# A low-rank adaptive layer and a recurrence on one core: the prologue from B2 on in another order, and x's first 64 steps on ScalarE's queue

## Chip, cores and metric

The kernel runs on one core of a Trainium2 chip. The metric is the device time of one execution in microseconds (us). Three timed runs of the kernel before gave a median of 525.01 us (524.35 to 525.34).

## What is computed

Four sequences (B = 4) of T = 512 steps and D = 256 features go through a layer whose low-rank factors are made from a condition vector, and then through a tanh recurrence; both add their input. The reference, cut to what matters (the layer's result takes the place of x ahead of the recurrence):

```python
c = layernorm(cond) * gamma + beta
w = gelu(c @ W1 + bias1) @ W2 + bias2                 # 4 x 8192
a1, b1, a2, b2 = [t.reshape(B, D, 8) for t in split(w, 4, axis=-1)]
u   = einsum('btd,bdr->btr', x, a2)
mid = gelu(x @ base_down + einsum('btr,blr->btl', u, b2))
v   = einsum('blr,btl->btr', b1, mid)
x   = x + (x + mid @ base_up.T + einsum('bkr,btr->btk', a1, v))
h_t = tanh(x_t @ Wx + b + h_(t-1) @ Wh)               # 512 steps, one after the other
out = x + h
```

## The kernel before

Every engine has a program written out by hand, and semaphores order them; there is no scheduler. The kernel has two stages.

**The recurrence** fills nearly all of the time. Two pairs of 16 steps (`PAIR` = 32) make one round; each step (`state_products`, L938) multiplies the state, split in three bf16 parts, by the parts of Wh in 24 matmuls, ScalarE takes the tanh (L494), VectorE makes the lower parts of the new state (`residue`, L579 and L583). In the gap in which TensorE would wait for the tanh stand other products: the layer for the next 32 steps (`fill_product`), the next inputs (`input_product`), transposes of x's rows. In the last 16 steps two matmuls (`x2_last_rows`, L862) put the last 8 rows of the layer's result where the output is summed; `X2_LAST` says from which step.

**The prologue** is all that must be done ahead of the first tanh (L494). It makes the four factors from W2, 8 MB, in the order A2, B2, B1, A1. For each factor j there are two halves c, and for each half two transfers k of 512 KB. `bias_product(j, c)` (L702) starts a bank with bias2; `w_products(j, c)` (L723) waits for the transfer of each k and adds 4 products, one for each strip of 32 partitions. VectorE's `keep_rank` (L559, L562) masks the result and reduces it to the compact factor `fac[j]`. A2 and B1 are turned by TensorE (`turn_factor`, L732). B2 and A1 are laid out by VectorE's `spread` (L566) as the block matrices `b2d` and `a1d` (128 x 256), from which a product of full height is made:

```python
nc.tensor.matmul(columns(bank[4 + n][:, 0:B * BL]), a1d[:, P * n:P * (n + 1)], v0_sb[:], start=False,
                 stop=True, skip_group_check=True).then_inc(up_psum, 1)
```

The order on TensorE is: x's first 64 steps transposed (`first_transposes`, L710, behind a wait for `ld_x[0]`), bias1 (L759), `cn` transposed (L763), the hidden layer (L773), x times base_down (L716), A2 and B2's products, u (L796), base_up turned (L802), the b2 products into mid (L808), B1's products, mid times base_up (L739), B1 turned, step 0 of the recurrence with h0 (L938), v (L743), A1's products, the a1 product (L749), the input products of the first tile (L831). `keep_busy(n)` (L689) puts n products of zeros, whose result nobody reads, between them.

All large loads are issued by SyncE (SP) on its queue, in the order x's first 64 steps, W1, base_down, A2, B2, Wh, base_up, B1, Wx, A1, and straight behind these x's other rows (`xb_sb` for steps 64 to 127, then three transfers of 512 KB, L317). Six small ones are issued by ScalarE.

Of the kernel before, what the change touches and what calls it, by code (L numbers as in the profile page):

```python
# [24 lines left out]
P = 128  # L25
# [7 lines left out]
def adaptive_lowrank_then_recurrence(nc, x, cond, base_up, base_down, ln_gamma, ln_beta, W1, bias1, W2,  # L33
# [25 lines left out]
    with ExitStack() as ctx:  # L59
# [240 lines left out]
        EARLY_SUMS, X2_LAST, EARLY_TURN, EARLY_ROWS = TS - LAST + 1, 9, 11, 12  # L300
# [12 lines left out]
        def _(sp):  # L313
# [11 lines left out]
            sp.dma_start(x_sb[0:T0, :, 0], x[:, 0:T0].rearrange("b p d -> p b d")).then_inc(ld_x[0], 16)  # L325
# [8 lines left out]
            load_w2(A1)  # L334

# [188 lines left out]
        def _(dve):  # L524
# [65 lines left out]
            keep_rank(B2, 0)  # L590
            spread(b2d, B2, 0).then_inc(b2d_ready, 1)
# [61 lines left out]

            def residues(pair, first, last):
                for s in range(PAIR):
# [28 lines left out]
        def _(pe):  # L684
# [33 lines left out]

            def w_products(j, c):
                for k in range(K2):  # L720
                    pe.wait_ge(ld_w2[j][c][k], 16)
                    for e in range(NCH):
                        last = nc.tensor.matmul(wbank(j, c)[Q * e:Q * (e + 1), :],  # L723
                                                gRep[:, k].rearrange("p b r -> p (b r)"),
                                                w2_sb[:, k, j, HC * (NCH * c + e):HC * (NCH * c + e + 1)], start=False,
                                                stop=(k == K2 - 1), skip_group_check=True)
                last.then_inc(w_ready[j], 1)
# [334 lines left out]
```

## Time and profile before

| what | us |
|---|---|
| three timed runs, median | 525.01 |
| the profiled execution's own time | 524.89 |
| its span, first to last instruction | 523.1 |
| first tanh of the recurrence | 37.44 |
| TensorE (PE) busy, share of the span | 505.3, 97% |
| VectorE (DVE) busy, share | 290.7, 56% |
| ScalarE (ACT) busy, share | 175.5, 34% |
| GpSimd (POOL) busy, share | 22.0, 4% |

The profile is of one execution. PE is TensorE's matmuls, PEld its weight loads, SPq and ACTq the issues of transfers by SyncE and ScalarE. Times in a trace count from the first instruction. A matmul in f32 is two instructions, so that `x16` in a row is 8 matmuls. A busy time of PE holds overlapping matmuls; the chain of waits gives what each group added.

### The profile page before, as it was taken

What the parts mean: (1) busy time and instruction counts of PE and PEld (TensorE: products, weight loads), DVE (VectorE), ACT (ScalarE), POOL (GpSimd) and SP (SyncE); (2) the same over time, 40 slices, a digit from 0 to 9 for tenths busy, and PEclk for the clock granted to TensorE, in tenths of its full rate; (3) what the DMA queues carried; (4) which work ended last, traced back from release to release, by engine and by line L of the source; (5) the groups of instructions that cost most, each with busy time, mean ns of one, the idle gap of its engine ahead of it and who ended that gap; (6) DMA issues with size and microseconds to landing.
All of it is one profiled execution on the core that took longest, in us unless ns stands there. A gap on an engine that the chain in (4) does not pass through costs nothing.

```text
span 523.1 us, 33150 instructions
## 1 busy us (share of the span) xinstructions
PE 505.3 (97%) x14760; PEld 471.2 (90%) x14760; DVE 290.7 (56%) x2274; ACT 175.5 (34%) x1159; POOL 22.0 (4%) x35
## 2 busy tenths in 40 slices
PE   9999999999999999999999999999999999998987
PEld 6569999999999999999999999999999999997885
DVE  2545565565556556555655555565655655565554
ACT  3103333333333333333333333333333333333322
POOL 7350000000000000000000000000000000000000
PEclk9999999999999999999999999999999999999999
DMA  8970000000000000000000000000000000000000
GB/s 295 398 217 4 4 14 4 5 14 4 14 5 14 4 9 11 4 14 4 15 4 14 4 5 14 5 14 4 14 4 4 14 4 14 4 14 4 5 14 13
DMA packets 8026, 16.05 MB, mean 31 GB/s; under 512 B 540, under 2 KB 5708, under 8 KB 7884
## 3 DMA queue, kind: packets, MB, share of 16 engines
q1 hardware_dynamic: 7816, 13.90, 7.8%
q8 instruction: 115, 1.88, 1.5%
q14 instruction: 27, 0.22, 0.1%
q10 hardware_dynamic: 68, 0.05, 0.0%
HBM read 11.85 MB, written 2.10 MB: 27 GB/s over the span
## 4 chain that ended last, share of the span: by engine, by line
PE 95%; ACT 3%; issue 1%; DVE 1%; POOL 0%; DVEq 0%; POOLq 0%
PE bank L938 64%; PE bank L842 7%; PE bank L904 4%; PE bank L885 4%; ACT h_ring L494 3%; PE bank L909 2%; PE bank L899 2%; PE bank L880 2%; PE bank L890 2%; PE bank L689 2%; PE bank L723 2%; PE bank L851 1%; PE bank L702 1%; PE bank L826 1%; PE bank L926 1%
## 5 line engine op out<-in xcount | busy, mean ns | idle before, releaser
L938 PE MATMUL bank<-h_ring,whp 128*128 128x52 bf16 x6132 | 243.6, 186 | 12.7 <-ACT h_ring L494 12.7
L579 DVE TENSOR_TENSOR r_ring<-h_ring 128x4 f32<-128x4 f32 x1022 | 136.0, 163 | 206.1 <-ACT h_ring L494 203.6
L494 ACT ACTIVATE h_ring<-bank 128x4 f32<-128x4 f32 x1022 | 141.9, 174 | 318.9 <-PE bank L938 311.1
L938 PEld LDWEIGHTS bank<-h_ring,whp 128*128 128x128 bf16 x6132 | 188.3, 96 | 34.7 <-ACT h_ring L494 25.7
L938 PE MATMUL bank<-r_ring,whp 128*128 128x52 bf16 x4096 | 219.5, 185 | 0.0
L938 PEld LDWEIGHTS bank<-r_ring,whp 128*128 128x128 bf16 x4096 | 173.6, 96 | 0.0
L938 PE MATMUL bank<-l_ring,whp 128*128 128x52 bf16 (+1 forms) x2048 | 156.4, 178 | 0.0
L583 DVE TENSOR_TENSOR l_ring<-r_ring 128x4 bf16<-128x4 f32 x1024 | 135.7, 162 | 0.0
L938 PEld LDWEIGHTS bank<-l_ring,whp 128*128 128x128 bf16 x2048 | 121.5, 96 | 0.0
L842 PE MATMUL bank<-xp,wxp 128*128 128x32 bf16 x1488 | 63.0, 176 | 0.0
L842 PEld LDWEIGHTS bank<-xp,wxp 128*128 128x128 bf16 x1488 | 50.5, 95 | 0.0
L904 PE MATMUL bank<-mid,upT 128*128 128x128 f32 x120 | 28.0, 316 | 0.0
L885 PE MATMUL bank<-xT,down_sb 128*128 128x128 f32 x112 | 26.2, 316 | 0.0
L826 PE MATMUL bank<-ones,b3h 128*128 128x32 bf16 x128 | 22.4, 176 | 0.0
L904 PEld LDWEIGHTS bank<-mid,upT 128*128 128x128 f32 x120 | 17.9, 188 | 0.0
L885 PEld LDWEIGHTS bank<-xT,down_sb 128*128 128x128 f32 x112 | 16.7, 188 | 0.0
L627 DVE TENSOR_TENSOR y_sb<-x2T,h_ring 128x64 f32<-128x64 f32 (+1 forms) x64 | 15.3, 279 | 0.0
L909 PE MATMUL bank<-v_sb,a1d 128*128 128x128 f32 x60 | 14.0, 316 | 0.0
L899 PE MATMUL bank<-mid,b1T 128*128 128x128 f32 x60 | 14.0, 316 | 0.0
L880 PE MATMUL bank<-xT,a2T 128*128 128x128 f32 x56 | 13.1, 316 | 0.0
L890 PE MATMUL bank<-u_sb,b2d 128*128 128x128 f32 x56 | 13.1, 316 | 0.0
L826 PEld LDWEIGHTS bank<-ones,b3h 128*128 128x128 bf16 x128 | 12.2, 96 | 0.2 <-issue 0.2
(134 smaller groups left out, 241.7 us busy)
## 6 DMA issues: line engine op xcount, KB each, us to landing
w_sb<-in_L_cond_W SPq DMA_DIRECT2D x16, 512.0 KB, 11.5
out<-o_sb SPq DMA_DIRECT2D x15, 128.0 KB
x_sb<-in_x SPq DMA_DIRECT2D x3, 512.0 KB, 15.6
x_sb<-in_x SPq DMA_DIRECT2D x1, 256.0 KB, 3.9
w_sb<-in_L_cond_W SPq DMA_DIRECT2D x1, 256.0 KB, 3.8
down_sb<-in_L_cond_base_down SPq DMA_DIRECT2D x1, 256.0 KB, 5.2
wh_sb<-in_L_cond_Wh SPq DMA_DIRECT2D x1, 256.0 KB, 11.4
up_sb<-in_L_cond_base_up SPq DMA_DIRECT2D x1, 256.0 KB, 11.6
```

The source lines that it names most:

```text
L494: nc.scalar.activation(state, zt, ACT.Tanh).then_inc(h_ready, 1)
L579: nc.vector.tensor_tensor(r_ring[:, k, q, 0:B], state_before(pair, s, k)[:, 0:B], state_hi_before(pair, s, k)[:, 0:B], ALU.subtract).then_ ...
L583: nc.vector.tensor_tensor(l_ring[:, k, q, 0:B], r_ring[:, k, q, 0:B], r_hi[:, k, q, 0:B], ALU.subtract).then_inc(l_ready, 1)
L826: nc.tensor.matmul(zbank(p, q, m)[:, 0:TC // 2], b3h[:, P * m:P * (m + 1)], ones[:], start=True, stop=False, skip_group_check=True)
L842: nc.tensor.matmul(zb, wxp[w][:, k, P * m:P * (m + 1)], rhs, start=False, stop=False, skip_group_check=True)
L880: ins = nc.tensor.matmul(columns(fill_out(tile, 0)), a2T[:, k].rearrange("p e q -> p (e q)"), xT[:, k, :, t0:t0 + BL], start=(k == 0), sto ...
L885: nc.tensor.matmul(columns(fill_out(tile, 1 + c)), down_sb[:, k, P * c:P * (c + 1)], xT[:, k, :, t0:t0 + BL], start=(k == 0), stop=False)
L890: nc.tensor.matmul(columns(fill_out(tile, 1 + c)), b2d[:, P * c:P * (c + 1)], u_sb[:], start=False, stop=True).then_inc(fmid_psum, 1)
L899: ins = nc.tensor.matmul(columns(fill_out(tile, 0)), b1T[:, k].rearrange("p e q -> p (e q)"), rhs, start=(k == 0), stop=(k == K2 - 1))
L904: nc.tensor.matmul(columns(fill_out(tile, 1 + c)), upT[:, k, P * c:P * (c + 1)], rhs, start=(k == 0), stop=False)
L909: nc.tensor.matmul(columns(fill_out(tile, 1 + c)), a1d[:, P * c:P * (c + 1)], v_sb[:], start=False, stop=True).then_inc(fup_psum, 1)
L938: return nc.tensor.matmul(zbank(p, q, m)[:, col0:col0 + n], whp[part][:, k, P * m:P * (m + 1)], rhs[:, 0:n], start=False, stop=stop, skip_ ...
```

## The change

1. x's first 64 steps are issued by ScalarE as its fourth transfer, not by SP as its first.
2. SP waits for A1's last two transfers ahead of x's other rows.
3. On TensorE 29 products of zeros (`keep_busy`) go from six places from B2 on, and 3 take the place of 7 ahead of B1's turning. The bias products of B1 and A1 no longer stand in pairs. B2's second half stands ahead of u and base_up's turning.
4. The first b2 and a1 products take the compact factor: `strip_products` makes 4 products of 32 rows by 32 columns in place of one of 128 by 128. The spreads of `a1d` and `b2d` stand in steps 3, 5, 6 and 7 of the recurrence on VectorE.
5. `state_products` is split in two; its second part for step 0 stands between A1's last products and the input products. The a1 product of the first half stands between A1's last two quarters.
6. `x2_last_rows` makes 64 columns at a time, in steps 3 to 6 of the last 16, not 128 in steps 9 and 10.

```diff
@@ -297,7 +297,7 @@
-        EARLY_SUMS, X2_LAST, EARLY_TURN, EARLY_ROWS = TS - LAST + 1, 9, 11, 12
+        EARLY_SUMS, X2_LAST, EARLY_TURN, EARLY_ROWS = TS - LAST + 1, 3, 11, 12
...
@@ -322,7 +322,6 @@
-            sp.dma_start(x_sb[0:T0, :, 0], x[:, 0:T0].rearrange("b p d -> p b d")).then_inc(ld_x[0], 16)
...
@@ -332,6 +331,9 @@
+
+            sp.wait_ge(ld_w2[A1][1][0], 16)
+            sp.wait_ge(ld_w2[A1][1][1], 16)
...
@@ -419,6 +421,7 @@
+            act.dma_start(x_sb[0:T0, :, 0], x[:, 0:T0].rearrange("b p d -> p b d")).then_inc(ld_x[0], 16)
...
@@ -587,26 +590,25 @@
-            keep_rank(B2, 0)
-            spread(b2d, B2, 0).then_inc(b2d_ready, 1)
+            for c in range(2):
+                keep_rank(B2, c)
             dve.wait_ge(u_psum, 1)
             nc.vector.tensor_tensor(u0_sb[:], bank[6][:, 0:B * T0].rearrange("p (b t) -> p b t", b=B),
                                     bmask[:].unsqueeze(2).broadcast_to([P, B, T0]), ALU.mult).then_inc(u_ready, 1)
-            keep_rank(B2, 1)
-            spread(b2d, B2, 1).then_inc(b2d_ready, 1)
             residue(0, 0)
-            keep_rank(B1, 0)
-            keep_rank(B1, 1)
+            for c in range(2):
+                keep_rank(B1, c)
             dve.wait_ge(b1T_psum, 2)
             nc.vector.tensor_copy(b1T[:, 1], turned(1)).then_inc(b1T_ready, 1)
+            keep_rank(A1, 0)
             dve.wait_ge(v0_psum, 1)
             nc.vector.tensor_tensor(v0_sb[:], bank[6][:, 0:B * BL].rearrange("p (b t) -> p b t", b=B),
                                     bmask[:].unsqueeze(2).broadcast_to([P, B, BL]), ALU.mult).then_inc(v0_ready, 1)
-            for n in range(K2):
-                keep_rank(A1, n)
-                spread(a1d, A1, n).then_inc(a1d_ready, 1)
-                dve.wait_ge(up_psum, n + 1)
-                make_x2(n, 0, TS).then_inc(x2_first, 1)
+            dve.wait_ge(up_psum, 1)
+            make_x2(0, 0, TS).then_inc(x2_first, 1)
+            keep_rank(A1, 1)
+            dve.wait_ge(up_psum, 2)
+            make_x2(1, 0, TS).then_inc(x2_first, 1)
...
@@ -650,6 +652,13 @@
+
+
+            PLACING = {3: (a1d, A1, 0, a1d_ready), 5: (a1d, A1, 1, a1d_ready), 6: (b2d, B2, 0, b2d_ready),
+                       7: (b2d, B2, 1, b2d_ready)}
+
+            def place(dst, j, c, done):
+                spread(dst, j, c).then_inc(done, 1)
...
@@ -665,6 +674,8 @@
+                    if tile == 0 and i in PLACING:
+                        place(*PLACING[i])
...
@@ -745,9 +759,17 @@
+
+            def strip_products(j, n, rhs, ncol, done):
+                for e in range(NCH):
+                    rows = slice(Q * e, Q * (e + 1))
+                    last = nc.tensor.matmul(columns(bank[4 + n][rows, 0:ncol]), fac[j][rows, n], rhs[rows], start=False,
+                                            stop=True, skip_group_check=True)
+                last.then_inc(done, 1)
+
             def a1_first_product(n):
-                nc.tensor.matmul(columns(bank[4 + n][:, 0:B * BL]), a1d[:, P * n:P * (n + 1)], v0_sb[:], start=False,
-                                 stop=True, skip_group_check=True).then_inc(up_psum, 1)
+                pe.wait_ge(fac_ready[A1], n + 1)
+                strip_products(A1, n, v0_sb, B * BL, up_psum)
...
@@ -785,39 +807,36 @@
-            keep_busy(4, 7)
             w_products(B2, 0)
             pe.wait_ge(fac_ready[A2], 2)
             turn_factor(A2, a2T_psum)
-            for c in range(2):
-                bias_product(B1, c)
+            bias_product(B1, 0)
+            w_products(B2, 1)
             pe.wait_ge(a2T_ready, 2)
             for k in range(K2):
                 last = nc.tensor.matmul(columns(bank[6][:, 0:B * T0]), a2T[:, k].rearrange("p e q -> p (e q)"),
                                         xT[:, k, :, 0:T0], start=(k == 0), stop=(k == K2 - 1))
             last.then_inc(u_psum, 1)
-            w_products(B2, 1)
             pe.wait_ge(ld_up, 16)
             for i in range(K2 * K2):
                 last = nc.tensor.transpose(bank[7][:, P * i:P * (i + 1)],
                                            up_sb[:, i % K2, P * (i // K2):P * (i // K2 + 1)], ident[:])
             last.then_inc(upT_psum, 1)
+            bias_product(B1, 1)
             pe.wait_ge(u_ready, 1)
             for m in range(K2):
-                pe.wait_ge(b2d_ready, m + 1)
-                nc.tensor.matmul(columns(bank[4 + m][:, 0:B * T0]), b2d[:, P * m:P * (m + 1)], u0_sb[:], start=False,
-                                 stop=True, skip_group_check=True).then_inc(mid_psum, 1)
-                keep_busy(4, 6)
+                pe.wait_ge(fac_ready[B2], m + 1)
+                strip_products(B2, m, u0_sb, B * T0, mid_psum)
             w_products(B1, 0)
-            for c in range(2):
-                bias_product(A1, c)
+            bias_product(A1, 0)
             pe.wait_ge(upT_ready, 1)
             for n in range(K2):
                 for k in range(K2):
                     pe.wait_ge(mid_ready, max(n, k) + 1)
                     base_up_product(n, k)
             w_products(B1, 1)
-            keep_busy(7, 7)
+            bias_product(A1, 1)
+            keep_busy(3, 6)
...
@@ -858,9 +877,10 @@
-            def x2_last_rows(k):
-                nc.tensor.matmul(last_rows(k), x2T[:, k, (T - LAST) * B:T * B], ident[:], start=True, stop=False,
-                                 skip_group_check=True)
+            def x2_last_rows(k, h):
+                cols = slice(P // 2 * h, P // 2 * (h + 1))
+                nc.tensor.matmul(last_rows(k)[:, cols], x2T[:, k, (T - LAST) * B:T * B], ident[:, cols], start=(h == 0),
+                                 stop=False, skip_group_check=True)
...
@@ -1011,28 +1038,24 @@
-            state_products(0, 0)
+            high_products(0, 0)
+            w_products(A1, 0)
             pe.wait_ge(b1T_ready, 2)
             for k in range(K2):
                 v0_product(k)
-            w_products(A1, 0)
-            keep_busy(6, 7)
+            w_half_products(A1, 1, 0)
             pe.wait_ge(v0_ready, 1)
-            pe.wait_ge(a1d_ready, 1)
             a1_first_product(0)
-            w_products(A1, 1)
+            w_half_products(A1, 1, 1)
+            rest_products(0, 0)
             pe.wait_ge(ld_wx, 16)
             pe.wait_ge(x2_first, 1)
             for m in range(K2):
                 first_input_product(0, m, 0)
-            bias_start(0, 1, 0)
-            first_input_product(1, 0, 0)
-            keep_busy(8, 7)
-            pe.wait_ge(a1d_ready, 2)
             a1_first_product(1)
-            bias_start(0, 1, 1)
-            first_input_product(1, 1, 0)
-            keep_busy(3, 7)
+            for m in range(K2):
+                bias_start(0, 1, m)
+                first_input_product(1, m, 0)
```

TensorE's order from B2's first products to those of B1's first half, before (`w_sb` is W2, `zeros` are the products of `keep_busy`, `b2d` the spread factor):

```order
L723 MATMUL bank<-w_sb,gRep 32x256 x8
L732 MATMUL bank<-ident,fac 32x128 x8
L702 MATMUL bank<-bias_sb,quadrant 128x256 x2
L796 MATMUL bank<-xT,a2T 128x256 x2
L723 MATMUL bank<-w_sb,gRep 32x256 x8
L802 MATMUL bank<-ident,up_sb 128x128 x4
L808 MATMUL bank<-u_sb,b2d 128x256
L689 MATMUL bank<-zeros 128x256 x4
L808 MATMUL bank<-u_sb,b2d 128x256
L689 MATMUL bank<-zeros 128x256 x4
L723 MATMUL bank<-w_sb,gRep 32x256 x8
```

and now (`fac` beside `u_sb` is the compact factor):

```order
L733 MATMUL bank<-w_sb,gRep 32x256 x8
L746 MATMUL bank<-ident,fac 32x128 x8
L713 MATMUL bank<-bias_sb,quadrant 128x256
L733 MATMUL bank<-w_sb,gRep 32x256 x8
L817 MATMUL bank<-xT,a2T 128x256 x2
L822 MATMUL bank<-ident,up_sb 128x128 x4
L713 MATMUL bank<-bias_sb,quadrant 128x256
L766 MATMUL bank<-u_sb,fac 32x256 x8
L733 MATMUL bank<-w_sb,gRep 32x256 x8
```

The 8 products of zeros in these rows are gone (so are 4 ahead of them); B2's second half has moved ahead of u, and the two b2 products have become 8 small ones in a row.

TensorE's order from A1's first products into the input products of the first tile, before (v, L743, stood ahead of these rows, and all of step 0 ahead of v):

```order
L723 MATMUL bank<-w_sb,gRep 32x256 x8
L689 MATMUL bank<-zeros 128x256 x6
L749 MATMUL bank<-v_sb,a1d 128x128
L723 MATMUL bank<-w_sb,gRep 32x256 x8
L831 MATMUL bank<-x2T,wx_sb 128x32 x2
L826 MATMUL bank<-ones,b3h 128x32
L831 MATMUL bank<-x2T,wx_sb 128x32
L689 MATMUL bank<-zeros 128x256 x8
L749 MATMUL bank<-v_sb,a1d 128x128
L826 MATMUL bank<-ones,b3h 128x32
L831 MATMUL bank<-x2T,wx_sb 128x32
L689 MATMUL bank<-zeros 128x256 x3
```

and now:

```order
L733 MATMUL bank<-w_sb,gRep 32x256 x8
L757 MATMUL bank<-mid,b1T 128x128 x2
L733 MATMUL bank<-w_sb,gRep 32x256 x4
L766 MATMUL bank<-v_sb,fac 32x128 x4
L733 MATMUL bank<-w_sb,gRep 32x256 x4
L958 MATMUL bank<-r_ring,whp 128x52 x6
L958 MATMUL bank<-l_ring,whp 128x52 x2
L958 MATMUL bank<-r_ring,whp 128x52 x2
L958 MATMUL bank<-l_ring,whp 128x52 x2
L850 MATMUL bank<-x2T,wx_sb 128x32 x2
L766 MATMUL bank<-v_sb,fac 32x128 x4
L845 MATMUL bank<-ones,b3h 128x32
```

The 17 products of zeros are gone, v stands behind A1's first half, A1's second half is cut by the first a1 product, and the second part of step 0 (L958) stands behind it. Only the first part of step 0 is still ahead of these rows.

VectorE's order from B1's turned half to the last of the layer's first result, before:

```order
L601 COPY b1T<-bank 128x128
L603 TENSOR_TENSOR v_sb<-bank,bmask 128x128
L559 TENSOR_TENSOR wmul<-bank,rmask 128x256
L562 TENSOR_REDUCE fac<-wmul 128x32
L566 TENSOR_TENSOR a1d<-fac,qmask 128x128
L571 SCALAR_TENSOR_TENSOR x2T<-xT,bank 128x4x16
L559 TENSOR_TENSOR wmul<-bank,rmask 128x256
L562 TENSOR_REDUCE fac<-wmul 128x32
L566 TENSOR_TENSOR a1d<-fac,qmask 128x128
L571 SCALAR_TENSOR_TENSOR x2T<-xT,bank 128x4x16 x3
```

and now:

```order
L602 COPY b1T<-bank 128x128
L562 TENSOR_TENSOR wmul<-bank,rmask 128x256
L565 TENSOR_REDUCE fac<-wmul 128x32
L605 TENSOR_TENSOR v_sb<-bank,bmask 128x128
L574 SCALAR_TENSOR_TENSOR x2T<-xT,bank 128x4x16
L562 TENSOR_TENSOR wmul<-bank,rmask 128x256
L565 TENSOR_REDUCE fac<-wmul 128x32
L574 SCALAR_TENSOR_TENSOR x2T<-xT,bank 128x4x16 x3
```

The two spreads stand no longer between a factor and its product, and A1's first factor is made ahead of `v_sb`.

## Rows read from the trace of the kernel before

**Rows 1.** The page, the chain that ended last: share of the span by line.

```profile
PE bank L938 64%; PE bank L842 7%; PE bank L904 4%; PE bank L885 4%; ACT h_ring L494 3%; PE bank L909 2%; PE bank L899 2%; PE bank L880 2%; PE bank L890 2%; PE bank L689 2%; PE bank L723 2%; PE bank L851 1%; PE bank L702 1%; PE bank L826 1%; PE bank L926 1%
```

**Rows 2.** Chain in order of time, prologue: start us, us, what.

```profile
6.30 0.64 PE bank L710 x8
...
15.62 0.54 PE bank L689 x4
16.16 1.00 PE bank L723 x16
17.16 0.44 PE bank L732 x16
17.60 1.06 PE bank L702 x4
18.66 1.06 PE bank L796 x4
...
25.74 1.09 PE bank L739 x8
...
34.72 0.56 PE bank L831 x4
```

**Rows 3.** Timeline, PE, the a1 product: start us, us, then what.

```profile
33.26 0.46 PE L749 MATMUL bank<-v_sb,a1d 128*128 128x128 f32 x2 [0.66 <-DVE a1d L566]
```

**Rows 4.** Timeline, ACT, the first tanh.

```profile
37.44 0.40 ACT L494 ACTIVATE h_ring<-bank 128x4 f32<-128x4 f32 x2 [7.78 <-PE bank L831]
```

**Rows 5.** Timeline, DVE, A1's second half.

```profile
35.25 0.42 DVE L562 TENSOR_REDUCE fac<-wmul 128x32 f32<-128x256 f32 x1
35.70 0.29 DVE L566 TENSOR_TENSOR a1d<-fac,qmask 128x128 f32<-128x128 f32 x1
36.67 0.53 DVE L571 SCALAR_TENSOR_TENSOR x2T<-xT,bank 128x64 f32<-128x64 f32 x3 [0.68 <-PE bank L749]
```

**Rows 6.** Timeline, SPq, issues of A1's second and last transfer.

```profile
15.12 1.47 SPq L322 DMA_DIRECT2D w_sb<-in_L_cond_W  x1
...
17.11 0.43 SPq L322 DMA_DIRECT2D w_sb<-in_L_cond_W  x1
```

**Rows 7.** DMA issues, us to landing: the same two; x's first 64 steps.

```profile
w_sb<-in_L_cond_W SPq DMA_DIRECT2D x1, 512.0 KB, 12.6
...
w_sb<-in_L_cond_W SPq DMA_DIRECT2D x1, 512.0 KB, 14.0
...
x_sb<-in_x SPq DMA_DIRECT2D x1, 256.0 KB, 3.9
```

**Rows 8.** Timeline, ACTq and POOL: the load of b on ScalarE's queue.

```profile
2.44 0.26 ACTq L423 DMA_DIRECT2D b_rows<-in_L_cond_b  x1
...
6.19 0.39 POOL L399 CAST b_part<-b_rows 3x256 bf16<-3x256 f32 x1 [1.88 <-DMA b_rows<-in_L_cond_b]
```

**Rows 9.** DMA queues, 5 to 6 us (q1 SP, q10 ScalarE): packets, MB, share.

```profile
q1 hardware_dynamic: 192, 0.33, 100.9%
q10 hardware_dynamic: 29, 0.03, 8.6%
```

**Rows 10.** Timeline, PE, the first products of zeros.

```profile
0.99 3.60 PE L689 MATMUL bank<-zeros 128*128 128x256 bf16 x16 [0.99 <-POOL zeros L364]
...
4.82 1.48 PE L689 MATMUL bank<-zeros 128*128 128x256 bf16 x12
```

**Rows 11.** Windows: us, PE, PEld, DVE, ACT, POOL busy, PEclk, DMA, GB/s.

```profile
5.07:13.00 7.93, 7.93 (x70) 6.11 (x67) 2.13 (x8) 2.16 (x7) 6.14 (x9) 1.00 1.03 394
```

**Rows 12.** Timeline, PE, the last steps.

```profile
512.05 0.47 PE L938 MATMUL bank<-h_ring,whp 128*128 128x52 bf16 x12 [0.17 <-ACT h_ring L494]
...
513.00 0.47 PE L938 MATMUL bank<-h_ring,whp 128*128 128x52 bf16 x12 [0.17 <-ACT h_ring L494]
...
513.70 0.41 PE L862 MATMUL bank<-ident,x2T 128*32 128x128 f32 x2
514.04 0.47 PE L938 MATMUL bank<-h_ring,whp 128*128 128x52 bf16 x12
```

More of the change, by code:

```diff
@@ L717, in base_down_product, with w_half_products @@
                                  start=(k == 0), stop=False, skip_group_check=True)
+            def w_half_products(j, c, k):
+                pe.wait_ge(ld_w2[j][c][k], 16)
+                for e in range(NCH):
+                    last = nc.tensor.matmul(wbank(j, c)[Q * e:Q * (e + 1), :], gRep[:, k].rearrange("p b r -> p (b r)"),
+                                            w2_sb[:, k, j, HC * (NCH * c + e):HC * (NCH * c + e + 1)], start=False,
+                                            stop=(k == K2 - 1), skip_group_check=True)
+                if k == K2 - 1:
+                    last.then_inc(w_ready[j], 1)
             def w_products(j, c):
                 for k in range(K2):
[L721 to L727, printed above, removed]
+                    w_half_products(j, c, k)
             def turn_factor(j, done):
@@ L908, in fill_product @@
                         pe.wait_ge(fv_ready, blk)
+                    if c == 0 and blk == 1:
+                        pe.wait_ge(a1d_ready, K2)
                     nc.tensor.matmul(columns(fill_out(tile, 1 + c)), a1d[:, P * c:P * (c + 1)], v_sb[:], start=False,
@@ L928, in turn_rows, with state_product, high_products, rest_products @@
                 last.then_inc(rows_psum, 1)
-            def state_products(pair, s):
+            def state_product(pair, s, part, k, m, rhs, stop=False):
                 p, q = s // TS, s % 2
                 col0 = B * (s % TS // 2)
+                n = B if stop else W
+                return nc.tensor.matmul(zbank(p, q, m)[:, col0:col0 + n], whp[part][:, k, P * m:P * (m + 1)],
+                                        rhs[:, 0:n], start=False, stop=stop, skip_group_check=True)
+            def high_products(pair, s):
+                for k in range(K2):
+                    pe.wait_ge(h_ready, 2 * PAIR * pair + 2 * s + k + 1)
+                    for m in range(K2):
+                        for part in range(NPART):
+                            state_product(pair, s, part, k, m, state_hi_before(pair, s, k))
+            def rest_products(pair, s):
+                q = s % 2
                 done = 2 * PAIR * pair + 2 * s
                 closes = not (pair == 0 and s == 0)
-                def product(part, k, m, rhs, stop=False):
-                    n = B if stop else W
-                    return nc.tensor.matmul(zbank(p, q, m)[:, col0:col0 + n], whp[part][:, k, P * m:P * (m + 1)],
-                                            rhs[:, 0:n], start=False, stop=stop, skip_group_check=True)
-                for k in range(K2):
-                    pe.wait_ge(h_ready, done + k + 1)
-                    for m in range(K2):
-                        for part in range(NPART):
-                            product(part, k, m, state_hi_before(pair, s, k))
                 pe.wait_ge(r_ready, done + 1)
@@ L959, in state_products @@
                 for part in range(2):
-                    product(part, 1, 1, r_hi[:, 1, q, :])
-                product(0, 0, 1, l_ring[:, 0, q, :])
-                ins = product(0, 1, 1, l_ring[:, 1, q, :], stop=closes)
+                    state_product(pair, s, part, 1, 1, r_hi[:, 1, q, :])
+                state_product(pair, s, 0, 0, 1, l_ring[:, 0, q, :])
+                ins = state_product(pair, s, 0, 1, 1, l_ring[:, 1, q, :], stop=closes)
                 if closes:
@@ L972, in recurrence @@
                     if not (first and s == 0):
-                        state_products(pair, s)
+                        high_products(pair, s)
+                        rest_products(pair, s)
                     else:
@@ L998, in recurrence @@
                             input_product(1 - p, n)
-                    if last and p == 1 and X2_LAST <= i < X2_LAST + K2:
-                        x2_last_rows(i - X2_LAST)
+                    if last and p == 1 and X2_LAST <= i < X2_LAST + 2 * K2:
+                        x2_last_rows(*divmod(i - X2_LAST, 2))
                     if last and p == 1 and EARLY_TURN <= i < EARLY_TURN + K2:
```

12 lines of the change are left out of this document (8 added, 4 removed).

## The prediction

> **What bounds the kernel now.** I read the chain of waits by line first: matmuls of the recurrence hold 64% of it [rows 1], and the change touches these in the last 16 steps only. So I went to the prologue, which is over with the first tanh at 37.44 us [rows 4], and read the chain there in order of time. TensorE is on it nearly throughout, and of that time some is products of zeros, which make nothing: 0.54 us for four [rows 2]. The rest of the chain is VectorE's, where a spread factor is waited for: the a1 product stood idle 0.66 us for it [rows 3]. Then I asked what holds the prologue once that goes: the transfers. A1's second transfer was issued at 15.12 and landed 12.6 later, at 27.7; its last at 17.11 plus 14.0, at 31.1 [rows 6, 7]. TensorE used that last one at 33.7 (34.72 less a group of 1.00 [rows 2]), so data was not yet the bound, but it is near.
>
> **The change part by part.**
>
> *x's first 64 steps.* TensorE waits for them at 6.30 [rows 2] and before that wait has nothing to spare. Before, they were first in SP's queue and landed 3.9 us after issue [rows 7]. Now ScalarE issues them one issue ahead of b's, so at about 2.1 [rows 8], in the midst of W1, base_down and A2. Lower end: 3.9 us again, 6.0, no wait. Upper end: b's 3 KB, issued at 2.44, came only at 6.19 [rows 8], 3.7 us; behind such a start x's 256 packets of 1 KB, 16 on each DMA engine, take turns with SP's. In 5 to 6 us the two queues ran side by side, 29 packets of q10 with 192 of q1 [rows 9]. If each of x's waits for one 4 KB packet of W2, the two move 16 x 16 x 5 KB = 1.3 MB, 3.3 us at 394 GB/s [rows 11], and land at 2.1 + 3.7 + 3.3 = 9.1. I take 7.7, near the middle: some of W1's and base_down's packets are as short as x's. TensorE then starts its transposes 1.4 us late, and all work of its own behind them moves by 1.4. ScalarE's issue itself (0.76 us for SP before) moves the statistics of the norm by as much; the wait for x covers it, and without that wait it would cost up to 0.76. bias1, b and bias2 land behind x; bias1 is needed two groups of TensorE work later, b only by GpSimd, which has Wh to wait for anyway.
>
> The Trainium skill, DMA: Bandwidth & Descriptors, "Queues, rings and completion order", says that an engine drains a packet of some 9 to 17 descriptors of one ring before it turns to the next; by that x would be through in a turn or two and the sum would be that of the first rival. The same page says that issuing from two engines saves only issue time, which the sum has as well.
>
> *The order from B2 on.* From 15.62 the work of TensorE up to A1's last product is now, with the groups of [rows 2]: six groups of W2 products at 1.00 = 6.0; four bias products at 0.53 = 2.1; two turnings at 0.44 = 0.9; u 1.06; base_up turned, half as much as the 1.09 of its product, 0.5; the b2 products, two at about 0.5, 1.0; mid times base_up 1.09; three products of zeros 0.4; the bias and first part of step 0, 12 matmuls, about 0.5 [rows 12]; v, half of u's columns, 0.5; the first a1 product 0.4 [rows 3]. Sum 14.4. Two short waits for VectorE stay (B1's factor ahead of its turning, v ahead of a1), 0.5 together. So A1's last product ends at 15.6 + 14.4 + 0.5 = 30.5, plus the 1.4 for x: 31.9.
>
> *The floor under it.* SP no longer issues x's other rows on A1's heels. Without them two more transfers of 512 KB take 1.3 us each at 394 GB/s, so A1's last lands at 27.7 + 2.7 = 30.4, not 31.1 [rows 6, 7, 11]; its four products then end at 30.9. That is 1.0 ahead of TensorE's own work: with x at 7.7 the data does not bind. It binds only if x costs less than 0.4.
>
> *Behind A1.* The last product ended at 34.72 [rows 2] and the tanh started at 37.44: 2.72. VectorE's factor (to 35.25 + 0.42 = 35.67 [rows 5]) takes 0.95; the spread of 0.29 goes, and with it what stood between it and the product; a1 about 0.4; from the result's first operation at 36.67 [rows 5] to the tanh 0.77, hardly shorter, since four input products (0.56 for two pairs [rows 2]) now stand there. About 2.25. The first tanh: 31.9 + 2.25 = 34.15, against 37.44 a gain of 3.3.
>
> *Moved to the recurrence.* Four spreads of 0.29 stand on VectorE in steps of 0.94 to 0.95 (512.05 to 513.00 [rows 12]), in which it is busy 56%; they stand behind the residues of their step, and the next tanh covers them. From nothing to 4 x 0.29 = 1.2 us; I take nothing, since that engine does as long an operation in other steps. Their readers are at step 8 and in the next 16. x's other rows are issued from 30.4; steps 64 to 127 should land 3.9 later [rows 7] with one more issue, at 35.2, and are wanted in step 4, 34.15 + 4 x 0.94 = 37.9: 2.7 spare. SP has nothing else to issue until the first output.
>
> *The end.* The two steps with an x2 product are 1.04 apart (513.00 to 514.04), not 0.95: that product keeps TensorE 0.34 from 513.70 [rows 12]. With 64 columns a quarter to a third of this goes, and the four steps fit: 0.2 us gained, at worst nothing.
>
> *Sum.* 3.3 + 0.2 = 3.5 us off the profiled execution of 524.89 (span 523.1 and 1.8 around it): 521.4. Its own time is 0.1 below the median of the timed runs, so I leave it there.
>
> **Rivals.**
> *x lands early, by 6.7.* For it: 3.9 us in the row of before. Then the data binds: tanh at 30.9 + 2.25 = 33.2, 4.4 us gained in all, 520.5. Against it: b's small load took 3.7 with 3 KB. Chance 0.14.
> *TensorE's clock falls in the wait for x.* Before, the granted clock was 1.00, the upper of the two levels of 2.4 and 1.2 GHz [rows 11], and TensorE never idled for over 0.7 us; the first 16 products of zeros took 3.60 us, the next 12 1.48 [rows 10], 0.225 against 0.123 each, so the lower level doubles a product. Now it stands for 1.4 us, soon after the clock rose, and 33 products of zeros are gone. Each microsecond of work done at the lower level costs one more. With half of the work up to the hidden layer (3.6 us) 1.8: 523.2; with all of it 525.0, no gain. Chance 0.14, a third of it at the far end.
> *The strips run one after another: slower.* The change makes a b2 or a1 product of four that differ in rows of the array as well as in columns. For their running together: 16 instructions of the W2 products, in four column strips, take 1.00, and four of full width with as many columns 1.06 [rows 2]. Strips that differ in rows this kernel has nowhere. The Trainium skill, TensorEngine Tiling (Array Packing), "Gotcha 1: PSUM Pressure", says that different row tiles cannot access the same PSUM bank at the same time, and here all four write one bank; by that rule this rival holds. In its favour from the rows: nothing; against it, that the strips write different partitions, as the column strips do. Price: a b2 product takes 4 x 0.53 = 2.1 for 0.5, an a1 product 4 x 0.27 = 1.1 for 0.4; 2 x 1.6 + 2 x 0.7 = 4.6 more. 521.4 + 4.6 = 526.0. It decides for slower from 3.5 us more on, so from about three quarters of that price. Chance 0.07.
> *The gain is taken elsewhere.* x at the late end, 9.1, and a spread or two not hidden: 1.4 + 0.6 more, 523.4; with VectorE's waits longer than 0.5 up to 524.8. Chance 0.07.
>
> **How the numbers follow.** The forecast with x between 6.9 and 8.4 has 0.58, and its own range is 520.7 to 522.3. A measurement can tell 0.2%, 1.05 us, from no change. Faster: 0.58 + 0.14 + two thirds of 0.14 + half of 0.07 = 0.85; within it: the rest of the clock and of the late cases, 0.08; slower 0.07. The range reaches down to the early case with 0.3 to spare, 520.2, and up past the late x and the short fall of the clock, 523.7; about 0.15 lies outside.
>
> **What would show it.** Right: TensorE idle ahead of x's transposes for 1 to 2 us with the transfer as releaser; the granted clock 1.00 behind it; eight strips of a b2 pair in about 1 us; A1's last transfer landed by 30.5 and used at once or 1 us later; first tanh at 34.2; the steps behind it still 0.94 apart, and no step of 1.04 near the end. Wrong: no idle there (first rival), matmuls twice as long behind it (second), strips with starts a full product apart (third), steps 3 to 7 longer than the others (fourth). Had the landing of A1 not moved ahead, SP's wait would not do what it is there for.

## The result, and the profile after

The changed kernel takes 535.94 us (median of six runs, 529.27 to 538.17), the kernel before beside it 524.69: a ratio of 1.019, 95% interval 1.0145 to 1.0237. It is slower by some 11 us, where 521.4 was forecast. The profiled execution took 534.91, its span is 533.1. One of the six, 529.27, was much faster than the others, with a mean clock of 0.99 for their 0.974 to 0.977, and every ratio here leaves out runs over 1.5% above their kernel's fastest, which is 538.17 here.

The chain in order of time of the changed kernel (start us, us, what), which answers to [rows 2]:

```profile
1.99 7.82 DMA x_sb<-in_x
9.80 0.04 issue
9.85 1.11 PE bank L721 x8
10.96 0.97 PE bank L700 x4
...
19.16 2.00 PE bank L713 x4
```

x's load was issued at 1.99 and landed 7.82 later, at 9.8, and with it TensorE's transposes start 3.5 us later than before. Behind it the groups take up to 1.9 times their old time: four products of zeros 0.97 instead of 0.54, two bias products (`x4` in f32) 2.00 instead of 1.06 [rows 2]. The page's two lines on the clock and the DMA in 40 slices of the span:

```profile
PEclk8588999999999999999999999999999999999999
DMA  8970000000000000000000000000000000000000
```

The clock is at half in the second slice and lower than before in the first, third and fourth. Windows of the changed kernel (us, busy of PE, PEld, DVE, ACT, POOL, then PEclk, DMA share, GB/s), for [rows 11]:

```profile
2.00:10.00 8.00, 5.21 (x28) 3.43 (x26) 2.64 (x9) 3.09 (x5) 2.24 (x6) 0.99 0.98 303
10.00:30.00 20.00, 20.00 (x111) 11.94 (x111) 2.51 (x6) 1.36 (x5) 14.27 (x19) 0.50 0.98 379
31.00:47.00 16.00, 15.73 (x202) 9.39 (x195) 6.84 (x25) 2.15 (x7) 3.13 (x1) 1.00 0.47 116
48.00:51.00 3.00, 3.00 (x55) 2.87 (x53) 1.44 (x10) 0.85 (x5) 0.00 (x0) 0.54 0.00 0
```

TensorE is busy for all 20 us from 10 to 30, at a granted clock of 0.50, the lower of its two levels (1.2 and 2.4 GHz). The DMA engines bring 379 GB/s in that time; A1 has landed by 30.8 us, when SP, which waits for it, issues x's next rows; it waits for TensorE, which takes the last of it at 43.4 us, not the other way round. From 31 us the clock is 1.00, and from 48 to 51 us it is low again, now in the recurrence. Timelines of the changed kernel, PE at three places, then ACT's first tanh, for [rows 4, 10]:

```profile
4.82 2.23 PE L700 MATMUL bank<-zeros 128*128 128x256 bf16 x12
9.85 1.11 PE L721 MATMUL bank<-ident,x_sb 64*128 64x64 f32 x8 [2.79 <-DMA x_sb<-in_x]
...
33.80 1.06 PE L766 MATMUL bank<-u_sb,fac 32*32 32x256 f32 x16
34.79 0.42 PE L733 MATMUL bank<-w_sb,gRep 128*32 128x256 f32 x4
...
47.17 0.57 PE L958 MATMUL bank<-h_ring,whp 128*128 128x52 bf16 x12
...
48.64 0.73 PE L958 MATMUL bank<-h_ring,whp 128*128 128x52 bf16 x12
...
50.26 0.69 PE L958 MATMUL bank<-h_ring,whp 128*128 128x52 bf16 x12
...
51.40 0.48 PE L958 MATMUL bank<-h_ring,whp 128*128 128x52 bf16 x12
```

```profile
46.40 0.40 ACT L497 ACTIVATE h_ring<-bank 128x4 f32<-128x4 f32 x2 [5.99 <-PE bank L850]
```

TensorE stood 2.79 us for x, from 7.05 on, and the clock fell at 9.8. The first tanh is at 46.40, not 37.44: 8.96 later. The three steps from 47.17 to 51.40 take 4.23 us, where three at 0.94 are 2.8: 1.4 more. The end gives back about 0.2. 8.96 + 1.4 - 0.2 = 10.2, and the spans differ by 10.0. So the loss lies in the prologue and in three steps at a low clock. What x's landing and the clock have to do with it, the runs below tell.

### The profile page after: what moved, and what is told of

Its sections match the earlier page's. It is cut to its first block, busy times and chain, and to the rows that moved or that the text cites. A ratio compares the mean times of both kernels' runs of the same rounds, so it can differ in the third digit from the quotient of the medians.

```text
span 533.1 us, 33147 instructions
## 1 busy us (share of the span) xinstructions
PE 513.9 (96%) x14755; PEld 475.2 (89%) x14755; DVE 290.3 (54%) x2274; ACT 175.8 (33%) x1159; POOL 21.9 (4%) x35
## 4 chain that ended last, share of the span: by engine, by line
PE 94%; ACT 3%; DMA 1%; issue 1%; DVE 0%; ACTq 0%
PE bank L958 63%; PE bank L861 7%; PE bank L926 4%; PE bank L905 3%; ACT h_ring L497 3%; PE bank L733 2%; PE bank L921 2%; PE bank L933 2%; PE bank L912 2%; PE bank L900 2%; DMA x_sb<-in_x 1%; PE bank L713 1%; PE bank L870 1%; PE bank L845 1%; PE bank L727 1%
## 5 line engine op out<-in xcount | busy, mean ns | idle before, releaser
L958 PE MATMUL bank<-h_ring,whp 128*128 128x52 bf16 x6132 | 243.9, 186 | 12.2 <-ACT h_ring L497 12.2
L958 PE MATMUL bank<-r_ring,whp 128*128 128x52 bf16 x4096 | 220.6, 186 | 0.0
L958 PEld LDWEIGHTS bank<-h_ring,whp 128*128 128x128 bf16 x6132 | 188.7, 96 | 33.6 <-ACT h_ring L497 24.6
L958 PEld LDWEIGHTS bank<-r_ring,whp 128*128 128x128 bf16 x4096 | 174.6, 96 | 0.4 <-issue 0.4
L958 PE MATMUL bank<-l_ring,whp 128*128 128x52 bf16 (+1 forms) x2048 | 157.3, 178 | 0.0
L958 PEld LDWEIGHTS bank<-l_ring,whp 128*128 128x128 bf16 x2048 | 122.4, 96 | 0.0
L900 PE MATMUL bank<-xT,a2T 128*128 128x128 f32 x56 | 13.1, 316 | 0.0
L912 PE MATMUL bank<-u_sb,b2d 128*128 128x128 f32 x56 | 13.1, 316 | 0.0
```

The source lines that it names most:

```text
L900: ins = nc.tensor.matmul(columns(fill_out(tile, 0)), a2T[:, k].rearrange("p e q -> p (e q)"), xT[:, k, :, t0:t0 + BL], start=(k == 0), sto ...
L912: nc.tensor.matmul(columns(fill_out(tile, 1 + c)), b2d[:, P * c:P * (c + 1)], u_sb[:], start=False, stop=True).then_inc(fmid_psum, 1)
L958: return nc.tensor.matmul(zbank(p, q, m)[:, col0:col0 + n], whp[part][:, k, P * m:P * (m + 1)], rhs[:, 0:n], start=False, stop=stop, skip_ ...
```

## The experiments

All intervals are of the ratio to the kernel before, run beside them. Twelve kernels ran.

### x back on SP's queue

```diff
-            act.dma_start(x_sb[0:T0, :, 0], x[:, 0:T0].rearrange("b p d -> p b d")).then_inc(ld_x[0], 16)
+            sp.dma_start(x_sb[0:T0, :, 0], x[:, 0:T0].rearrange("b p d -> p b d")).then_inc(ld_x[0], 16)
             sp.dma_start(w1_sb[:], W1.rearrange("(k p) n -> p k n", p=P)).then_inc(ld_w1, 16)
```

> The changed kernel with x's first 64 steps back at the head of SP's queue, nothing else. Theory: the whole loss comes from x landing at 9.8 us, TensorE standing 2.8 us for it and its clock falling to the lower level; with x back no idle over 0.3 us at x's transposes, granted clock 1.00 throughout, first tanh at 33.0 to 33.6 us, time 520.2 to 521.2. Rival 1, the removal of the products of zeros from B2 on lets the clock fall anyway: granted clock 0.5 somewhere between 16 and 37 us and a time of 522 to 530. Rival 2, the strips or the new order are slow in themselves: first tanh not before 35 us at clock 1.00.

Measured: 522.30 us (521.69 to 524.08), ratio 0.9948 (0.9935 to 0.9961). A window, the timeline of PE at two places and ACT's first tanh:

```profile
5.00:33.00 28.00, 27.40 (x313) 16.37 (x311) 11.57 (x33) 4.09 (x12) 17.08 (x20) 1.00 0.88 337
```

```profile
6.28 0.71 PE L721 MATMUL bank<-ident,x_sb 64*128 64x64 f32 x8
...
40.25 0.38 PE L941 MATMUL bank<-ident,xb_sb 128*128 128x128 f32 x2 [1.02 <-issue]
```

```profile
33.93 0.40 ACT L497 ACTIVATE h_ring<-bank 128x4 f32<-128x4 f32 x2 [6.01 <-PE bank L850]
```

With this one transfer moved back, TensorE waits for nothing at x's transposes, the clock is 1.00 through the prologue, and the change is a gain of 3 us. Everything else in the change is innocent of the loss. The tanh is 3.5 us earlier than before, 0.3 later than the latest I expected, and the time is a microsecond above what I expected. Most of that is the second row: 1.02 us at 39.2 to 40.25 in which TensorE waited for nothing that the profile shows.

### Only x's load moved, in the kernel before

```diff
-            sp.dma_start(x_sb[0:T0, :, 0], x[:, 0:T0].rearrange("b p d -> p b d")).then_inc(ld_x[0], 16)
...
             act.dma_start(beta_sb[:], ln_beta.partition_broadcast(B)).then_inc(ld_gb, 16)
+            act.dma_start(x_sb[0:T0, :, 0], x[:, 0:T0].rearrange("b p d -> p b d")).then_inc(ld_x[0], 16)
```

> The kernel before with only x's load moved to ScalarE's queue, behind beta. Theory: this alone brings the loss; x lands at about 9.8, TensorE idles 2.8 us, the clock falls to 0.5 at about 10 us, and the time is 533 to 545, more than the changed kernel's, since the prologue's order is the long one. Rival, the products of zeros of before from B2 on bring the clock back early: half clock for under 7 us and a time of 528 to 533. Rival, the loss needs the new order too: clock 1.00 and 528 to 529, x's 3.5 us alone.

Measured: 533.60 us, ratio 1.0179 (1.0144 to 1.0215). PE's timeline and windows:

```profile
10.52 1.11 PE L710 MATMUL bank<-ident,x_sb 64*128 64x64 f32 x8 [3.20 <-DMA x_sb<-in_x]
```

```profile
10.10:20.20 10.10, 9.68 (x39) 7.64 (x40) 0.81 (x2) 1.09 (x4) 6.66 (x10) 0.51 1.04 397
20.40:45.00 24.60, 23.74 (x271) 14.60 (x270) 10.24 (x29) 1.78 (x5) 11.55 (x10) 1.00 0.68 220
```

The one line brings a loss of 8 us by itself. x came at 10.5, and the clock was low for 10 us in this execution, not for 20. It was back by 20.6 us, in the middle of A2's bias products, ahead of the first place at which the two programs differ on TensorE, so the removed products of zeros are not what decides between 10 and 20. Within each kernel the runs differ too (mean clock 0.99 in three of four here, 0.981 in one; 0.974 to 0.977 in five of six of the changed kernel, 0.99 in the run of 529.27). The length goes in jumps, and what picks it stays open.

### The wait for x filled with products of zeros

```diff
-            keep_busy(12)
+            keep_busy(40)
```

> The changed kernel, x still on ScalarE's queue, with 40 products of zeros instead of 12 ahead of the wait for x, so that TensorE is busy until about 9.8 us. It tells the wait's own length from the clock's fall. Theory, the clock is most of the loss: granted clock 1.00 all through, first tanh at about 36.3 us (32.75 plus 3.5 for x), time 523 to 524.5. Rival, the lateness of x and its train is the loss: time stays above 530.

Measured: 525.41 us (524.28 to 535.38 in ten runs), ratio 1.0010 (0.9995 to 1.0024), without the run of 535.38. PE's timeline, a window, and ACT's first tanh:

```profile
4.82 4.54 PE L700 MATMUL bank<-zeros 128*128 128x256 bf16 x40
10.54 0.71 PE L721 MATMUL bank<-ident,x_sb 64*128 64x64 f32 x8 [1.19 <-DMA x_sb<-in_x]
```

```profile
10.00:37.00 27.00, 26.19 (x304) 15.84 (x304) 9.07 (x28) 2.88 (x9) 18.43 (x20) 1.00 0.88 313
```

```profile
37.64 0.40 ACT L497 ACTIVATE h_ring<-bank 128x4 f32<-128x4 f32 x2 [6.00 <-PE bank L850]
```

x came at 10.5, later than in the changed kernel, and yet the clock held and 10 us came back. The tanh and the time are about a microsecond above what I expected, in part since x came 0.7 later than I took. This parts the loss: x's lateness costs about 3 us against x_on_sp, the clock's fall the rest. Products of zeros do not make it safe: of ten runs one took 528.7 and one 535.4, with a mean clock of 0.994 and 0.98. The stop that is left is 1.19 us in the profiled execution, near the 1.4 of the forecast; the stops of those two runs are not known.

### TensorE idle with x early

```diff
+            pe.wait_ge(ld_w2[A2][0][1], 16)
             pe.wait_ge(ld_x[0], 16)
             first_transposes(0)
```

> As x_on_sp, so x is early, but TensorE waits for A2's second transfer (9.9 us) ahead of x's transposes, where the changed kernel waits for x (9.8 us). No transfer is moved. It tells TensorE's idleness from x's lateness and its queue. Theory, the idle stretch alone lets the clock fall: 0.5 from about 10 us for 10 to 20 us, time 530 to 537. Rival, the late x or the second queue does it: clock 1.00 and 525 to 526.

Measured: 535.82 us, ratio 1.0205 (1.0191 to 1.0218). x is on SP's queue here and no transfer is moved.

```profile
10.06 1.11 PE L721 MATMUL bank<-ident,x_sb 64*128 64x64 f32 x8 [3.75 <-DMA w_sb<-in_L_cond_W]
```

```profile
6.40:8.20 1.80, 0.00 (x0) 0.00 (x0) 0.49 (x3) 0.00 (x0) 1.57 (x4) 1.00 1.02 397
8.40:35.40 27.00, 25.34 (x135) 14.89 (x136) 4.08 (x12) 1.36 (x5) 16.61 (x17) 0.50 0.89 330
```

3.75 us of idleness, and the clock is at the lower level for 27 us, the loss of the changed kernel over again. It is TensorE's standing still that does it, not the second queue. The clock fell at 8.3, 2.0 us into the stop, and not at its end.

The same with A2's first transfer (`ld_w2[A2][0][0]`) and with base_down's (`ld_down`):

> The same with A2's first transfer (about 8.7 us): some 2 us of idleness, between idle_until_down and idle_until_a2 (535.8). Theory, it is a matter of how long TensorE stood: mostly fallen, 529 to 536. Rival, only the full 2.8 us do it: clock 1.00, 523.5 to 525.

> As x_on_sp, with TensorE waiting for base_down (about 7.4 us) ahead of x's transposes: about 1 us of idleness, near the 1.4 us that the forecast gave the changed kernel. Theory: so short a stop leaves the clock at 1.00 and costs at most its own length, 522.3 to 523.5. Rival: the clock falls here too, 528 or more, and the forecast would have failed even with x as early as it said.

Measured: the first, median 532.9, but its four runs took 523.38, 531.42, 534.38 and 534.39, with mean clocks of 0.999, 0.984, 0.977 and 0.977; the second 523.15, ratio 0.9959 (0.9945 to 0.9974), clock 1.00 in all four. The profiled execution of the first is its fastest run, that of the second is one of four alike:

```profile
8.54 0.71 PE L721 MATMUL bank<-ident,x_sb 64*128 64x64 f32 x8 [2.26 <-DMA w_sb<-in_L_cond_W]
```

```profile
4.82 2.17 PE L700 MATMUL bank<-zeros 128*128 128x256 bf16 x12
7.18 0.71 PE L721 MATMUL bank<-ident,x_sb 64*128 64x64 f32 x8 [0.19 <-DMA down_sb<-in_L_cond_base_down]
```

After 2.26 us of idleness the clock held once. It fell in the three other runs, whose stops no profile shows: the same program goes one way or the other. The run with base_down missed its aim. I took base_down to land at 7.4 and the zeros to end at 6.3; in this execution the 12 products of zeros took 2.17 us, since the clock rose late at the start, and TensorE stood only 0.19. It shows that so little does nothing, but not what the 1.4 us of the forecast would have done; no run settles that.

### x as ScalarE's second transfer

```diff
             act.dma_start(cond_sb[:], cond).then_inc(ld_cond, 16)
+            act.dma_start(x_sb[0:T0, :, 0], x[:, 0:T0].rearrange("b p d -> p b d")).then_inc(ld_x[0], 16)
             act.dma_start(gamma_sb[:], ln_gamma.partition_broadcast(B)).then_inc(ld_gb, 16)
```

> The changed kernel with x as ScalarE's second transfer, issued at about 1.35 us and not 1.99. Theory, x is late because it takes turns packet by packet with SP's: its packets would start near 3.5 us beside W1's and base_down's of 1 KB and land at 7.0 to 8.2; the norm's gamma and beta come behind it. TensorE idles about 1 us, the clock mostly holds, 522 to 524, with runs above 530 where it does not. Rival, a transfer of ScalarE's takes 7.8 us wherever it stands: x at 9.2, clock fallen, 533 or more.

Measured: 529.0 us, with seven runs from 523.77 (clock 1.00) to 536.26 (0.974); the ratio of the four below 530 is 1.0048 (1.0013 to 1.0084). The profiled execution is one of the others, 534.47. Its row of PE, two windows, its DMA issue of x, and below it the queues of the changed kernel from 5 to 8 us (packets, MB, share):

```profile
10.42 1.07 PE L721 MATMUL bank<-ident,x_sb 64*128 64x64 f32 x8 [4.58 <-DMA x_sb<-in_x]
```

```profile
3.80:10.40 6.60, 2.04 (x18) 1.41 (x16) 2.05 (x7) 3.09 (x5) 1.86 (x4) 1.00 0.94 298
10.60:30.90 20.30, 20.30 (x111) 12.21 (x111) 2.37 (x8) 1.36 (x5) 13.69 (x17) 0.50 0.94 366
```

```profile
x_sb<-in_x ACTq DMA_DIRECT2D x1, 256.0 KB, 9.0
```

```profile
q1 hardware_dynamic: 209, 0.77, 75.2%
q10 hardware_dynamic: 207, 0.21, 21.4%
```

Both theories missed the landing: issued 0.65 us earlier, x took 9.0 us and came at 10.4, and TensorE stood 4.58 us for it, not 1. The clock was 1.00 to 10.4 through all of this stop, and low for the 20 us behind it. The rows of the changed kernel show the turns: 209 packets of SP's queue and 207 of ScalarE's in the same 3 us, one for one, with 3.7 KB in one of SP's and 1 KB in one of x's. Equal counts alone would allow longer turns too, but the packets' own times in the trace do not: from 5 to 8 us a data packet starts 3 or 4 ns ahead of the end of one of the other queue 329 times, of one of its own queue 50 times. At that rate x's 256 packets need 3.7 us, and that part of the theory holds. But issued earlier x did not land earlier: from 3 to 6 us its queue moved 204 packets, as fast as in the changed kernel, and then the last ones trickled, 26 to 37 in each microsecond from 6 to 10. Which engines hold them back the views do not show, so the lateness of the tail is open. Against the kernel before (256 KB in 3.9 us on SP's queue [rows 7]) a load that is wanted first took 7.8 to 9.0 on the other queue.

The Trainium skill, DMA: Bandwidth & Descriptors, "Queues, rings and completion order", speaks of packets of some 9 to 17 descriptors drained in one turn; by the 209 to 207 packets here the turns are of one packet, and 16 of x's, not one or two, stand behind SP's on each engine. The measurement decides.

### Zeros behind x

```diff
             first_transposes(1)
-            keep_busy(4)
+            keep_busy(28)
```

> The changed kernel with 28 products of zeros instead of 4 behind x's transposes. It asks what keeps the clock low for 20 us. Theory, the small f32 products behind x do not bring it back as dense bf16 products do: the clock rises within 7 us of its fall instead of 20, and the time is 528 to 532 in spite of 3 to 5 us of added work. Rival, it comes back when it will: half clock for 20 us as before and 538 or more.

Measured: 529.56 us, ratio 1.0086 (1.0069 to 1.0103).

```profile
9.00:13.00 4.00, 3.18 (x19) 2.45 (x20) 0.00 (x0) 0.74 (x2) 1.86 (x4) 0.59 1.03 386
13.00:40.00 27.00, 26.73 (x306) 16.31 (x304) 10.25 (x27) 2.23 (x7) 16.57 (x17) 1.00 0.86 300
```

24 more products that nobody reads make the changed kernel 6 us faster. The clock fell as before, at 9.7, but among dense bf16 products it was back by 13.1 us, while in the changed kernel, with TensorE just as continuously busy, for the most part with narrow and small f32 products, it stayed low until 30.3. So a busy TensorE in the profile is not by itself what brings the clock back. Here rows and page differ: the Trainium skill, TensorE: Matmul & The Clock Gate, Part 1, lets the clock rise when the engine is busy; the changed kernel's PE was busy 20.00 of 20.00 us at 0.50.

### What the parts are worth

The zeros alone, taken from the kernel before (its six places of `keep_busy` from B2 on, and 3 for 7):

> The kernel before with the products of zeros from B2 on taken out as the change does, and nothing else. Theory, the clock does not need them as long as TensorE has its own work: granted clock 1.00 and 1.0 to 2.5 us faster than before, 522.7 to 524.2. Rival, the clock falls without them: granted clock 0.5 for some stretch of the prologue and 526 or more.

The spreads back in the prologue, with x on SP:

```diff
-                pe.wait_ge(fac_ready[A1], n + 1)
-                strip_products(A1, n, v0_sb, B * BL, up_psum)
+                pe.wait_ge(a1d_ready, n + 1)
+                nc.tensor.matmul(columns(bank[4 + n][:, 0:B * BL]), a1d[:, P * n:P * (n + 1)], v0_sb[:], start=False,
+                                 stop=True, skip_group_check=True).then_inc(up_psum, 1)
```

> As x_on_sp, with the spreads of b2d and a1d back in the prologue and the b2 and a1 products of full size; prices the strips. Theory, the strips run together and only the spread's 0.3 and the wait behind it are saved: first tanh 0.3 to 0.9 us later than x_on_sp's 33.93. Rival, strips are slower than full products: no later, or earlier.

SP's wait taken out, with x on SP:

```diff
-            sp.wait_ge(ld_w2[A1][1][0], 16)
-            sp.wait_ge(ld_w2[A1][1][1], 16)
```

> As x_on_sp, and SP issues x's other rows straight behind A1, as before. It prices SP's wait. Theory: with x early the prologue's end hangs on A1's last transfer, which lands at 31.1 instead of 30.4, so 0.5 to 0.8 us slower than x_on_sp. Rival, TensorE's own work is the bound: no difference (within 0.2).

And steps 64 to 127 issued ahead of that wait:

```diff
+            sp.dma_start(xb_sb[:].rearrange("p r d -> p (r d)"),
+                         x[:, T0:P].rearrange("b (q r) d -> b q (r d)", r=2)).then_inc(ld_xb, 16)
             sp.wait_ge(ld_w2[A1][1][0], 16)
             sp.wait_ge(ld_w2[A1][1][1], 16)
```

> As x_on_sp, but the 256 KB of x's steps 64 to 127 are issued straight behind A1 and ahead of SP's wait; only the other three transfers wait. In x_on_sp TensorE stood 1.02 us in step 4 for these rows. Theory: the stall goes and A1's last transfer still lands early, first tanh 33.9 to 34.4 us, time 520.7 to 521.3, better than both x_on_sp (522.3) and x_on_sp_no_sp_wait (521.6). Rival, the stall is not a late transfer: it stays at about 1 us and the time at 522.3.

| kernel | median us | ratio, 95% interval | first tanh us |
|---|---|---|---|
| zeros removed only | 524.64 | 0.9996 (0.9977 to 1.0015) | 37.41 |
| x on SP, spreads back | 522.84 | 0.9956 (0.9943 to 0.9970) | 34.59 |
| x on SP | 522.30 | 0.9948 (0.9935 to 0.9961) | 33.93 |
| x on SP, no wait of SP | 521.56 | 0.9929 (0.9916 to 0.9942) | 35.06 |
| x on SP, 64 to 127 ahead of the wait | 521.67 | 0.9932 (0.9920 to 0.9945) | 34.32 |

The first tanh is read from one execution of each kernel, and it depends on when TensorE could begin: with x on SP the first transposes stand at 6.75, 6.28, 6.91 and 7.22 us in the order of the table, by when the products of zeros ahead of them ended.

*Zeros.* No gain that can be told: their places were filled by the wait for VectorE's spread, here 1.42 us for 0.66 [rows 3]. And of ten runs three took 526.0 to 527.5 with clocks of 0.993 to 0.997. Without them the clock of this order holds in most runs only.

```profile
33.33 0.46 PE L749 MATMUL bank<-v_sb,a1d 128*128 128x128 f32 x2 [1.42 <-DVE a1d L566]
```

*Strips.* The b2 pair and the last a1 product, first of x_on_sp, then of spreads_back, in their chains (start us, us, what):

```profile
21.39 0.99 PE bank L766 x16
...
32.60 0.42 PE bank L766 x8
```

```profile
21.36 1.13 PE bank L831 x4
...
32.95 0.30 DVE a1d L569
...
33.29 0.49 PE bank L773 x2
```

Two b2 products in strips take 0.99 us, an a1 product 0.42; the full ones take 1.13 and 0.49. The spread of 0.30 goes, and 0.4 us per product on the path with what stands around it. In the timed runs the two intervals overlap, so the 0.5 us between the medians is not settled by them. The Trainium skill's rule on row tiles and one PSUM bank (TensorEngine Tiling (Array Packing), "Gotcha 1: PSUM Pressure") does not hold back strips that write different partitions of the bank: 16 instructions in 0.99.

*SP's wait.* It does what it is there for: without it TensorE waits 0.93 us for A1's last transfer.

```profile
32.09 0.64 PE L730 MATMUL bank<-w_sb,gRep 128*32 128x256 f32 x8 [0.93 <-DMA w_sb<-in_L_cond_W]
```

The time is not what I expected: the tanh is 1.1 us earlier with the wait, the median 0.7 longer, and the two intervals touch. The 1.02 us stop of x_on_sp takes back what the tanh gains. I had read it as a wait for steps 64 to 127; but these rows' first transposes ran at 38.1, a step earlier, so the transfer had landed, and the stop lies between two matmuls with no releaser. The DMA queues of x_on_sp from 38 to 40 us, and then of xb_ahead_of_wait from 36 to 38 (from 38 to 40 it has none):

```profile
q1 hardware_dynamic: 431, 0.43, 67.0%
q14 instruction: 1, 0.01, 1.4%
```

```profile
q1 hardware_dynamic: 188, 0.18, 28.4%
q8 instruction: 1, 0.02, 3.8%
```

In x_on_sp x's other rows were still moving, at 9.1 us from issue to landing, when packets of the program itself (the instruction queues q8 and q14) were due. In xb_ahead_of_wait they were through by 38 us, and its profile has no such stop; nor has that of x_on_sp_no_sp_wait. Those of idle_until_down and spreads_back, with x's rows as late as in x_on_sp, have one of 1.29 and one of 0.55 us. But idle_until_a2_first and filled_wait, with these rows as late, have only 0.31 and 0.28, and zeros_behind_x none. That TensorE waited for its own instructions behind x's rows may be, but it is not shown. With steps 64 to 127 ahead of the wait the stop goes, as expected, and the time is that without the wait, 0.4 above my range. So SP's wait brings nothing that the timed runs can tell.

Both last versions beat the kernel before by 0.7% and the changed kernel by 2.6% (0.9929 against 1.0191).

## Why the prediction was wrong

**x's landing.** The step "I take 7.7, near the middle" failed: it was 9.8, past even the upper end of 9.1. The turns were priced about right (3.3 for 3.7). x's packets set in ahead of 5 us, not at 5.8 (17 of the queue from 4 to 5), and a tail of late packets was priced at nothing: 73 of the queue, the last of x's among them, ran from 8 to 10. This term alone moves the time by 2.1.

**"TensorE's clock falls in the wait for x."** This was a rival at 0.14, priced at 1.8 to 3.6 us. Its mechanism is what happened, and both its chance and its price failed. The chance: it was weighed for a stop of 1.4 us; the stop was 2.79, and with one set at some 2.3 us the clock already fell in three of four runs. The price: it was laid on "the work up to the hidden layer", as if the clock came back once TensorE had work. It stayed low from 9.8 to 30.3. From x's transposes to the first tanh filled_wait, whose clock held, took 27.10 us (10.54 to 37.64), the changed kernel 36.55 (9.85 to 46.40): the fall cost 9.45, less than half of the 20.5, as the groups took less than twice their time. The forecast had 26.45 there (7.7 to 34.15), 0.65 too little. 9.45, 0.65 and 2.15 for x are the 12.25 by which the tanh came late. The second fall, 1.4 in three steps, was in no rival. With it the sum is 13.65, and the profiled execution is 13.5 above the forecast.

**The rest of the sum.** The order from B2 on was priced a little low: with x on SP, A1's last product ended at 31.64, where the sum without x's 1.4 says 30.5 and its floor 30.9. Bias products took 0.62, not 0.53, and TensorE stood 0.33 us for B2's last transfer, a wait that the sum left out. The tanh came 2.3 us behind it (2.25 forecast). A1's last transfer landed by 31.0 there, when SP issued x's next rows, and not at 30.4; that did not bind. *The end:* the four half products of x2 fit, steps of 0.94; the timeline of x_on_sp, to set beside [rows 12]:

```profile
505.03 0.48 PE L958 MATMUL bank<-h_ring,whp 128*128 128x52 bf16 x12 [0.17 <-ACT h_ring L497]
505.74 0.30 PE L882 MATMUL bank<-ident,x2T 128*32 128x64 f32 x2
505.97 0.48 PE L958 MATMUL bank<-h_ring,whp 128*128 128x52 bf16 x12
```

*Moved to the recurrence:* the spreads cost nothing, as taken: but for the stop, the steps of x_on_sp that hold them are 0.94 apart. "SP has nothing else to issue" was true, but x's other rows, moved behind A1, go together with a stop of 1 us in x_on_sp that the sum did not have. *The strips* run together: the rival for "slower" was the wrong one. The rival named for a late x at 9.1 was closest on the landing and left out that the clock hangs on it: two rivals were kept apart that are one chain.

## What to carry to other kernels

A wait that TensorE has not had before is priced twice: by its length, and by what the clock does behind it, which can be several times the length and lasts as long as the work behind it does not bring it back. Before a load is moved to another queue, ask who it then takes turns with: the first thing that the critical engine wants belongs alone at the head. If one must wait, dense products of zeros up to the landing are cheap: 28 more of them took back 10 of the changed kernel's 11 us, in eight runs of ten.

## What the runs showed of the hardware

- The granted clock fell in or just behind stops of 2.79, 3.20, 3.75 and 4.58 us in the profiled executions, and held through stops of 1.19 and 2.26. The length alone does not say when: it fell 2.0 us into the stop of 3.75, and only at the end of that of 4.58. It then stayed at 0.50 for 10, 20 or 27 us with TensorE busy.
- Having fallen at 9.7 us, it was back at 13.1 among 28 dense bf16 products. Behind a fall at about 10 us with narrow f32 products it was back at 20.6 us in one kernel and at 30.3 in another.
- It can fall again without idleness that the rows show: from 48 to 51 us in the changed kernel, 1.4 us lost in three steps. No run here tells why.
- Two hardware queues share a DMA engine packet for packet (209 to 207), whatever the packet's size, so that a queue of 1 KB packets beside one of mostly 4 KB gets a fifth of the bytes.
- The same 12 products of zeros at the start took 1.48 to 2.50 us from one profile to the next, by when the clock first rose; this moves what stands behind them by up to 1 us, and may be part of the runs' spread.
